# Local attention: DVE takes the feed-forward's statistics behind the first group's subtraction of the maximum, not ahead of the third table product

## The reference, cut to what matters

```python
for i in range(DEPTH):                       # DEPTH = 6
    x = attn_layer(shift_tokens(x), Wqkv[i], q_scale[i], k_scale[i], Wo[i]) + x
    x = ffn_layer(shift_tokens(x), ln_g[i], ln_b[i], W1[i], b1[i], W2[i], b2[i]) + x
# attn_layer: q, k, v = split(x @ Wqkv); q, k = l2norm(q) * qs, l2norm(k) * ks
#             rotary tables on q and k; softmax over windows of 32 (the own and the one before); @ Wo
# ffn_layer:  xn = (x - mean) / sqrt(var + 1e-5) * g + b
#             a, gate = split(xn @ W1 + b1); (a * gelu(gate)) @ W2 + b2
```

## Time and profile before

| | before |
|---|---|
| median of 3 runs | 2269.71 us (2268.53 to 2270.89) |
| the profiled execution | 2269.04 us, span 2267.3 us |
| mean granted PE clock | 0.984 |
| busy, of the span | PE 93%, DVE 81%, ACT 73%, POOL 73%, PE weight loads 63% |

### The profile page before, as it was taken

The page is one execution under the profiler, slowest core; times in us unless marked ns, Lnnn a source line. Parts: engine busy times, 40 slices in busy tenths (PEclk is TensorE's granted clock), DMA queues, the critical chain, the costliest instruction groups (busy, mean ns, idle before and its releaser), DMA issues. The chain is left out here.

```text
span 2267.3 us, 70752 instructions
## 1 busy us (share of the span) xinstructions
PE 2108.9 (93%) x26387; PEld 1429.3 (63%) x26387; DVE 1840.3 (81%) x2681; ACT 1662.4 (73%) x3300; POOL 1653.9 (73%) x1553
## 2 busy tenths in 40 slices
PE   5898769999979999999999999999999999999995
PEld 3555436666546676766667666666666666666674
DVE  4898957777788888888888888888888888888883
ACT  5888845454367788788788878878877787887773
POOL 4667843332378888888888888888888888888881
PEclk8999989999999999999999999999999999999997
DMA  2321220000023223222322322232232222223221
GB/s 76 110 65 64 65 73 2 1 1 1 1 52 78 70 60 79 69 71 67 82 71 56 83 69 70 69 77 76 56 83 70 70 69 73 77 59 83 70 64 47
DMA packets 103501, 140.43 MB, mean 62 GB/s; under 512 B 63376, under 2 KB 64400, under 8 KB 103056
## 3 DMA queue, kind: packets, MB, share of 16 engines
q1 hardware_dynamic: 103440, 139.64, 23.1%
HBM read 56.39 MB, written 1.31 MB: 25 GB/s over the span
## 5 line engine op out<-in xcount | busy, mean ns | idle before, releaser
L1727 PE MATMUL f_psA<-f_W,f_xT 128*128 (+1 forms) x1154 | 599.4, 615 | 8.9 <-ACT f_Vt L1479 3.6
L1617 DVE TENSOR_TENSOR f_m<-f_psA,f_tab 128x1024 f32<-128x1024 f32 x385 | 458.4, 1212 | 62.9 <-ACT f_sq L1461 62.9
L1397 POOL TENSOR_TENSOR f_qkr<-f_qkr,f_rn 128x1024 f32<-128x1024 f32 x192 | 361.2, 1902 | 17.2 <-POOL f_rn L1420 17.2
L1368 POOL TENSOR_TENSOR f_Pr<-f_Pr,f_rden 128x384 f32<-128x384 f32 x384 | 307.7, 833 | 74.4 <-DVE f_rden L1606 74.4
L1461 ACT ACTIVATE f_sq<-f_psA 128x512 f32<-128x512 f32 x385 | 222.0, 589 | 103.9 <-PE f_psA L1727 100.2
L1727 PEld LDWEIGHTS f_psA<-f_W,f_xT 128*128 128x128 f32 x1154 | 191.6, 189 | 129.5 <-issue 88.4
L1387 POOL TENSOR_TENSOR f_qkr<-f_m 128x512 f32<-128x512 f32 x192 | 243.6, 1269 | 18.9 <-DVE f_m L1617 18.9
L1388 POOL TENSOR_TENSOR f_qkr<-f_m 128x512 f32<-128x512 f32 x192 | 245.6, 1279 | 0.0
L794 POOL TENSOR_TENSOR x_Es<-x_E 128x512 f32<-128x512 f32 x64 | 81.0, 1266 | 205.9 <-DVE x_E L899 205.9
L1593 DVE TENSOR_REDUCE f_mx<-f_psS 128x8 f32<-128x768 f32 x192 | 183.4, 955 | 50.0 <-PE f_psS L1762 50.0
L1648 DVE TENSOR_REDUCE f_ssq<-f_sq 128x32 f32<-128x2048 f32 x96 | 218.5, 2276 | 0.0
(11 more groups left out here) (176 smaller groups left out, 4717.1 us busy)
## 6 DMA issues: line engine op xcount, KB each, us to landing
f_V<-f_Vt SPq DMA_DIRECT2D x96, 384.0 KB, 4.2
f_V<-f_Vt SPq DMA_DIRECT2D x96, 256.0 KB, 3.5
f_W<-in_f_W SPq DMA_DIRECT2D x48, 344.0 KB, 3.0
m_Cb<-m_BC_rows SPq DMA_DIRECT2D x64, 256.0 KB, 3.1
f_W<-in_f_W SPq DMA_DIRECT2D x48, 296.5 KB, 3.5
f_V<-f_Vt SPq DMA_DIRECT2D x48, 128.0 KB, 4.3
f_xsA<-xall SPq DMA_DIRECT2D x98, 32.0 KB
f_xsA<-xall SPq DMA_DIRECT2D x98, 31.8 KB
```

The lines of the kernel that those rows point to most:

```text
L1368: pool.tensor_tensor(pv, pv, rv.unsqueeze(3).broadcast_to([P, 2, 2, KEYS]), ALU.mult).then_inc(Pr_ready[g][j], 1)
L1397: pool.tensor_tensor(qv, qv, rv.unsqueeze(3).broadcast_to([P, 2, GH, DH]), ALU.mult).then_inc(qkr_ready[g], 1)
L1617: dve.tensor_tensor(m12[:, j, :, half].rearrange("p m (h d) -> p m h d", d=DH), psA[n % 2][:, :].rearrange("p (h d) -> p h d", d=DH).unsqu ...
L1727: pe.matmul(psA[n % 2][:, :], xT[:, t, :], weights(i, W_QKV + n * 512, 512), start=True, stop=True).then_inc(A_full[n_fill], 1)
```

## The change

In DVE's slot the block of stage c, with its two waits and two instructions, stands behind the third table product, the sum of squares, and the first group's maximum and subtraction, and ahead of the next tile's table product. Other engines are as they were.

```diff
                 if "E" in stages:
                     gated(2)
+                if "A" in stages:
+                    table_products(u, t, 2)
+                    dve.tensor_reduce(ssq[:, :], sq[:, :].rearrange("p (h d) -> p h d", d=DH), axis=AX.X, op=ALU.add).then_inc(ssq_ready, 1)
+                if "B" in stages:
+                    maximum(v, 0)
+                    less_maximum(v, 0)
                 if "c" in stages:
                     dve.wait_ge(xsC_ready[q], (i - q) * (32, 48)[q])
                     dve.bn_stats(out=statC[:, :], in_=xsC[:, q, :]).then_inc(dve_chain, 1)
                     at_least(dve, hatC_ready, done)
                     dve.wait_ge(dve_chain, done + 1)
                     alone(dve, passed)
                     dve.bn_aggr(out=momC[:, :], in_=statC[:, :]).then_inc(momC_ready, 1)
-                if "A" in stages:
-                    table_products(u, t, 2)
-                    dve.tensor_reduce(ssq[:, :], sq[:, :].rearrange("p (h d) -> p h d", d=DH), axis=AX.X, op=ALU.add).then_inc(ssq_ready, 1)
-                if "B" in stages:
-                    maximum(v, 0)
-                    less_maximum(v, 0)
                 if "A" in stages:
                     table_products(u + 1, 1 - t, 1)
```

## The result

The changed kernel takes 2308.83 us (median of 4 runs, 2302.67 to 2312.51), the kernel before 2269.12 us. The ratio is 1.0171, with a 95% interval of 1.0148 to 1.0195: slower by 1.7%, some 40 us. The forecast was 2300 us, in a range of 2286 to 2322. The profiled execution took 2309.93 us (span 2308.1), 40.9 more than the profiled one of before.

The account below looks back on a forecast made before the run. The prediction took PE to bound the loop, 291.8 of 300 us busy. Terms: 46 slots x 0.62 = 28.5, 47 x 0.1 = 4.7, first slot -2, together +31 on 2269.04, so 2300 us; range 2286 to 2322.

Parts of the forecast that it names:

- The bound: Attention and feed-forward loop: runs at PE's pace, busy 291.8 of 300 us; its time moves when PE's gaps move.
- (a): DVE's third table product, t=0: starts 0.65 us earlier, winning 0.30 of PE's 0.56 us gap at the scores.
- (b): DVE behind the subtraction: next table product 0.24 us late in t=0, second maximum starts as before; cost 0.
- (c): Late momC through ACT, POOL and hatC, t=0: transpose L1881 0.62 us late; bounds 0.3 better, 0.2 worse.
- (d): ACT's late evacuations at output projection L1892: 0.1 us a turn in t=1; 0, at most 0.12, in t=0.
- (e): POOL's queue: hatC and the q/k scaling behind it end later, within POOL's idle time; cost 0.
- (f): Loop's first slot: about 1.6 us of PE's 1.93 us gap and the slow clock's 1.05 go; -2 us, once.
- (1): Faster: late momC is hidden at transpose L1881, only (a) and (f) are left; 2253 us, chance 0.08.
- (2): No change: PE makes up the 0.62 us later in the turn; about 2269 us, chance 0.05.
- (3): Evacuations decide at the output projection, (d) at its bounds: 15 us more, 2315 us, chance 0.07.
- (4): PE's clock falls at two close gaps in each t=0: 1.05 us a turn, 48 us more, 2348 us, chance 0.06.
- The sum: Whole kernel: 28.5 us from t=0, 4.7 from t=1, -2 from the first slot; +31 us, so 2300 us.

Follow-up runs that it names:

- e3: Changed kernel with the statistics in t=0 one place later still, behind the next tile's table product: 2395.92 us, ratio 1.0539 to the kernel before.
- e7: Changed kernel with neither PE nor ACT waiting for momC, the rows' normalisation left out: 2254.65 us, ratio 0.9912 to the kernel before.
- e2: Kernel before, with the statistics late in slots with t=1 only: 2270.62 us, ratio 0.9994.
- e5: Changed kernel with PE transposing the identity at L1881, not waiting for hatC: 2298.27 us, ratio 1.0107 to the kernel before.
- e6: Changed kernel with ACT taking a constant's logarithm without waiting for momC, POOL waiting for momC itself: 2278.79 us, ratio 1.0021 to the kernel before.
- e4: Kernel before, with the statistics moved behind the third table product and sum of squares, but ahead of the first maximum: 2263.92 us, ratio 0.9957.

## Why the prediction was right, point by point

- The bound. Right: a longer gap of PE came through in the turn, 1.14 us for 1.14 in e3's turns at full clock.
- (a), 0.30 us won at the scores: 0.29 by the timelines. The hand-over that I had chosen between 0 and 0.25 was the right one, as DVE's row shows (maximum 0.08 behind the scores' end at 1439.50).
- (b), cost nothing: right in the sum, but for another reason than "starts as before". Taken from the first group's scores, the second maximum in t = 0 starts at 4.54 us and before at 4.50. But PE's second group now starts 0.29 earlier, and from its mask product the maximum comes after 1.42 us (1441.79 to 1443.21), before after 1.09. These 0.33 us would be felt if PE went on without a wait: e7 loses 0.11 a turn by them. Here the wait at the transpose covers them.
- (c), the transpose 0.62 late: 0.75. This is the term that was sized too small. From bn_stats to the transpose it is 1443.78 - 1441.44 = 2.34 us where the tail had shown 2.21. The pair of statistics is 0.43 apart and not 0.40, and from `hatC`'s start to the transpose it takes 0.94 us; in the tail of the changed kernel 0.84, as its rows show:

```profile
2288.66 0.79 POOL L1412 TENSOR_SCALAR f_hatC<-f_xsC,f_momC,f_rstdC 128x128 f32<-128x128 f32 x1 [6.64 <-ACT f_rstdC L1538]
...
2289.50 0.69 PE L1881 MATMUL f_psD<-ident,f_hatC 128*128 128x128 f32 x2 [7.21 <-POOL f_hatC L1412]
```

  This, and not the number of slots or the path, is the term of the sum that was off: 0.75 where I had 0.62. Over 46 slots 0.12 to 0.13 us are 6 of the 9 us by which 2300 was too low. The bound of 0.2 worse held it.
- (d), 0.1 a turn in t = 1: 0.08 in the changed kernel, but 0 when it is alone (e2). So the 0.1 was right partly by luck. For t = 0 I had the projection's cost at 0, "at most 0.12". The number was right, the reasoning only half: I gave ACT's hand-over no time, and by that the evacuation seemed to be ready 0.3 us before the projection wants to start. In e5 it takes 0.29, so the two waits are about level. Whoever had removed the one at the transpose on the strength of my sum would have won next to nothing. The time itself isn't a constant: in t = 1 of the changed kernel the load starts 0.07 after the evacuation's end (1461.76 to 1461.83). Why t = 0 takes longer, no run shows.
- (e), POOL's queue: right. Its waits ahead of `hatC` grew by 104 us in total, and in the loop no instruction of PE waits for POOL's other work.
- (f), the first slot: the gap of 1.93 us is gone, the clock stays up, and 1.13 us lie between transpose and projection where it was 2.19:

```profile
694.14 0.36 PE L1751 MATMUL f_psS<-f_maskb,f_same_row 64*64 64x384 bf16 x4 [0.27 <-DVE f_Pr L1598]
696.14 0.43 PE L1881 MATMUL f_psD<-ident,f_hatC 128*128 128x128 f32 x2 [0.98 <-POOL f_hatC L1412]
697.27 1.97 PE L1892 MATMUL f_psO<-f_W,f_oT 128*128 x16
```

- The rivals. (1), faster: its point of decision was a path of 1.59 us, and it is 2.34. Its gain was put too high as well: with neither PE nor ACT held (e7) a turn is 0.18 shorter, not 0.30. (2), no change by a PE with time to spare: against it stand e3, where 1.14 us of lateness cost 1.14 in the turns at full clock, and e6. For this kernel the rule of the Trainium skill ("Perfetto Trace Analysis", Identifying the Most-Contended Engine) doesn't decide how a late start on PE is felt: weight loads fill 62% of the span after the change, yet nothing is made up. (The section names the share of peak arithmetic, MFU, beside the load share; nothing here measures it.) (3), evacuations: not what sets the time, but level with what does. (4), the clock: in the loop of the changed kernel it stayed at 1.00 in each stretch of 300 us. The gap of 0.98 left the clock alone, e3's 2.12 did not. Rival (4) is real one step further on, at 1.46 us in every second turn.
- The sum. 0.74 x 46 + 0.08 x 47 - 2 = 36 us by measured terms. The execution's 40.9 has some 4 more, from the last L1502 to the end: 62.7 us after (2245.4 to 2308.1) against 58.9 before (2208.4 to 2267.3), where PE's clock stood at 0.59 in the last 38 us of the one and 0.68 in the last 37 of the other. The traces of the other kernels speak against the change as its cause: e2 and e4, which lose nothing, have 62.6 and 63.1 us there, e5 has 60.1, and e7, with the statistics as late as in the changed kernel, 58.0. Why the tail differs from one to the next stays open. Of the 10 us by which the profiled execution lies above 2300, some 4 are the tail's and 6 are (c)'s.

## What to carry to other kernels

When a small instruction is moved back on the engine that makes it, follow its result and not its duration. Here 0.54 us of work was moved behind 5.4 us of other work, and the cost was set by the path of 2.34 us that its result takes through two other in-order queues, with everything that stands behind the waiting instruction on those queues as a second path. If an instruction waits early for its input but its consumer is near, move it just past the work that needs not wait, and no further: that place (e4) gave 0.12 of the 0.29 us a turn at none of the price. And before one of two waits with a common cause is removed, work out where the other ends, with the hand-over in it.

## What the runs showed of the hardware that I had not expected

- A gap of 2.12 us in an otherwise full PE halved its clock in every second turn of 36 us, a gap of 0.98 with one of 0.27 close before it never in the changed kernel's loop (clock 1.00 in each stretch of 300 us). The mean alone, 35.85 us a turn, would have hidden that there are two kinds of turn.
- From the end of an ACT evacuation to the start of the matmul that needs it PE took 0.29 us in e5 (1405.32 to 1405.61), to the weight load in t = 0 of the changed kernel 0.30 (1444.53 to 1444.83), but in t = 1 only 0.07. DVE's start after ACT's square takes 0.02 to 0.03 (in the changed kernel 1435.90 to 1435.92).

```profile
1444.83 1.86 PEld L1892 LDWEIGHTS f_psO<-f_W,f_oT 128*128 128x128 f32 x16 [0.58 <-issue]
```
